# Attention of a two-layer transformer block: probabilities transposed by DMA as two 16-bit planes, and 16-bit values

## What is computed

```python
q = rope(rms_norm(x @ wq)); k = rope(rms_norm(x @ wk)); v = x @ wv          # 16 query heads, 4 key heads, 128 wide
k_full = concat(rms_norm(ctx @ wk_ctx), k); v_full = concat(ctx @ wv_ctx, v) # 512 keys, the last 256 causal
probs = softmax(q @ k_full.T / sqrt(128) + causal)
x = x + (probs @ v_full) @ wo
x = x + ffn0(layernorm(x)); x = x + topk_attention(...); x = x + gated_ffn(...)
```

## Time and profile before

| | |
|---|---|
| median of 3 runs | 1545.7 us (1543.1 to 1548.31) |
| profiled execution | 1547.26 us, span 1546.0 us |
| granted TensorE clock | 0.993 of full speed |
| PE busy | 1488.8 us, 96% |
| DVE busy | 1137.2 us, 74% |
| ACT busy | 959.3 us, 62% |
| POOL busy | 692.1 us, 45% |
| first attention | from the start to about 877 us |

### The profile page before, as it was taken

The page is one execution under the profiler, slowest core; times in us unless marked ns, Lnnn a source line. Parts: engine busy times, 40 slices in busy tenths (PEclk is TensorE's granted clock), DMA queues, the critical chain, the costliest instruction groups (busy, mean ns, idle before and its releaser), DMA issues. The chain is left out here.

```text
span 1546.0 us, 26210 instructions
## 1 busy us (share of the span) xinstructions
PE 1488.8 (96%) x8644; PEld 1165.6 (75%) x8644; DVE 1137.2 (74%) x2966; ACT 959.3 (62%) x2470; POOL 692.1 (45%) x832
## 2 busy tenths in 40 slices
PE   7899999999999999999999999999998899999988
PEld 6778888888888888888888666666666566666653
DVE  6787677777776877777788765555566898888774
ACT  5666666666666656666667765555546577666655
POOL 4564555464645555555567300000015455555544
PEclk9999999999999999999999999999999999999999
DMA  7011111111111111111144789778866301111000
GB/s 281 28 42 55 42 69 42 42 69 42 56 56 42 69 42 42 69 42 56 57 190 177 263 288 292 260 248 261 260 210 203 99 9 54 56 49 42 28 14 28
DMA packets 84327, 165.09 MB, mean 107 GB/s; under 512 B 39392, under 2 KB 39520, under 8 KB 82784
## 3 DMA queue, kind: packets, MB, share of 16 engines
q1 hardware_dynamic: 84192, 163.41, 30.8%
HBM read 113.05 MB, written 41.94 MB: 100 GB/s over the span
## 5 line engine op out<-in xcount | busy, mean ns | idle before, releaser
L617 ACT ACTIVATE Pt<-Pt,small 128x384 f32<-128x384 f32 (+1 forms) x256 | 172.7, 682 | 106.1 <-DVE small L877 106.0
L368 PE MATMUL bank<-wq,xT 128*128 128x512 f32 x768 | 206.7, 404 | 1.0 <-DVE wq L772 1.0
L421 PE MATMUL bank<-PT,vv 128*128 128x512 f32 x672 | 199.6, 405 | 4.7 <-DVE PT L862 3.8
L1135 POOL TENSOR_SCALAR Pt<-Pt,small 128x384 f32<-128x384 f32 (+1 forms) x256 | 164.0, 653 | 79.0 <-DVE small L885 78.9
L877 DVE CUSTOM_DVE_ANT_0 Pt<-quad,mask,small 128x384 f32<-128x384 f32 (+1 forms) x256 | 171.6, 679 | 30.7 <-PE quad L398 29.4
L1356 PE MATMUL bank<-wq,ot 128*128 128x512 f32 x768 | 182.1, 395 | 1.5 <-DMA ot<-ot_scratch 1.5
L862 DVE TENSOR_TENSOR PT<-quad,PT 128x512 fp32r<-128x512 f32 x224 | 153.6, 686 | 37.9 <-ACT PT L609 37.5
L1356 PEld LDWEIGHTS bank<-wq,ot 128*128 128x128 f32 x768 | 143.9, 188 | 33.7 <-DMA ot<-ot_scratch 2.2
L368 PEld LDWEIGHTS bank<-wq,xT 128*128 128x128 f32 x768 | 136.8, 189 | 26.4 <-DVE wq L772 2.3
L1123 POOL TENSOR_TENSOR t<-t 128x512 f32<-128x512 f32 x64 | 83.6, 1306 | 144.1 <-DVE t L843 144.1
L421 PEld LDWEIGHTS bank<-PT,vv 128*128 128x128 f32 x672 | 116.4, 189 | 28.9 <-DVE PT L862 10.2
(11 more groups left out here) (286 smaller groups left out, 3502.6 us busy)
## 6 DMA issues: line engine op xcount, KB each, us to landing
ot_scratch<-OT SPq DMA_DIRECT2D x64, 512.0 KB, 2.9
ot<-ot_scratch SPq DMA_DIRECT2D x64, 512.0 KB, 5.7
wkv_f<-in_w SPq DMA_DIRECT2D x12, 512.0 KB, 6.5
wkc_f<-in_w SPq DMA_DIRECT2D x12, 512.0 KB, 6.9
wkv_f<-in_wg SPq DMA_DIRECT2D x11, 512.0 KB, 6.9
wkv_f<-in_wd SPq DMA_DIRECT2D x11, 512.0 KB, 6.6
wkv_f<-in_wu SPq DMA_DIRECT2D x10, 512.0 KB, 7.1
stg<-in_ctxT SPq DMA_DIRECT2D x16, 256.0 KB, 4.1
```

The costliest lines, as they stand in the source:

```text
L368: ins = pe.matmul(bQ[:], xT[p][:, k, qt * 128:qt * 128 + 128], wq[j][:, g, k, :], start=(part == 0 and k == 0), stop=(part == 2 and k == 3))
L421: ins = pe.matmul(bO[:], vv[x][:, bg % 2, kt, :], PT[y][:, k % 2, :], start=(kt == 0 and n == 0), stop=(kt == tiles_in(i) - 1 and n == 2))
L617: act.activation(p, p, ACT.Exp, bias=nm[:, i % 2, h:h + 1], scale=-1.0, accum_out=sm[:, i % 2, h:h + 1]).then_inc(f["s_exp"], 1)
L1135: pool.tensor_scalar(p, p, ri[:, i % 2, h:h + 1], 1.0, ALU.mult, ALU.mult).then_inc(f["p_n"], 1)
```

## The change

The normalised probabilities are no longer transposed by TensorE. pool_norm now multiplies E (one buffer, where Pt had two) by 2^15 over the row sum and writes a float16 plane; dve_p_lo writes the remainder E times the same factor minus that plane as a second float16 plane, per head, both inputs in SBUF. For each block, SP issues one DMA transpose per plane for all heads (sp_p_turn: 12 or 16 tiles of 128 by 128) into PT. The two planes are one buffer each (planes), so pool_norm of a block's head 0 waits for t_hi, the landing of the block before's high transpose, and dve_p_lo of head 0 for t_lo, that of the low one. pe_pv then runs over the whole block in three parts, high plane first, low plane last. The values vv are float16 planes too, scaled per group by a factor sig that is worked out from the sums of squares of weights and of x's context (act_square, pe_scale, dve_scale, pool_scale, dve_unscale) at steps 0, 2, 4 and once per batch; act_o and dve_o_lo undo the scale. Scores rotate over three PSUM banks, bS, where there were two; the fourth bank of quad goes to even units of keys and values. Further: dve_k_n moves to ACT (act_k_n), dve_ln_b to POOL (pool_ln), dve_ri gets a second small instruction and a wait between the two, even and odd steps get one common order, dve_k_lo and dve_q stand at the end of dve_step behind the four dve_p_lo, and the product with the last attention blocks (pe_y) is placed anew around steps 62 and 63.

```diff
-    bS = [quad[:, 0, :], quad[:, 1, :]]
-    bP = [quad[:, 2, :], quad[:, 3, :]]
+    bS = [quad[:, j, :] for j in range(3)]
...
-    vv = [sb(st, f"vv{j}", [128, 2, 4, 128], F32R) for j in range(2)]
+    vv = sb(st, "vv", [128, 2, 2, 4, 128], F16)
...
-    Pt = [sb(st, "Pt0", [128, 4, 384], F32), sb(st, "Pt1", [128, 4, 512], F32)]
+    E = sb(st, "E", [128, 4, 512], F32)
+    PT = [sb(st, "PT0", [128, 24, 128], F16)]
...
+    def scales(i):
+        if i in (0, 2, 4):
+            return i // 2, 0, (0, 1, 2)[i // 2] + (i > 0), 2 if i == 0 else 1
+        return 2 + (i + 2) // 8, (i + 2) // 8, 0, 4
+    def scaled(i):
+        return i in (0, 2, 4) or i % 8 == 6 and i + 2 < NBLK
...
+    def sp_p_turn(i, x):
+        n = tiles_in(i)
+        if x == 0:
+            after(sp, f["pv_mm"], i - 1)
+        sp.wait_ge(f[("p_n", "p_lo")[x]], 4 * i + 4)
+        sp.dma_start_transpose(PT[i % 2][:, 4 * n * x:4 * n * x + 4 * n, :],
+                               planes[:, x, 0:4 * width(i)]).then_inc((t_hi, t_lo)[x], 16)
...
-        for i in range(1, NBLK + 1):
+        for i in range(NBLK + 2):
             b, r = divmod(i, 8)
-            p = i - 1
+            if i >= 2:
+                p = i - 2
+                sp.wait_ge(f["o_lo"], p + 1)
+                sp.dma_start(ot_dram[2 * (p // 8) + p % 2, p // 2 % 4], OT[:].bitcast(F32)).then_inc(f["ot0"], 16)
+            if i == 62:
+                sp.wait_ge(f["xt_mm"], NT)
+                sp.wait_ge(f["q_rope"], NBLK)
+                sp.wait_ge(f["k_rope"], NU // 2)
+                sp.wait_ge(f["q_mm"], NBLK)
+                sp.wait_ge(f["kv_mm"], NU)
+                sp.wait_ge(f["ot0"], 16 * 56)
+                for c in range(2):
+                    ffn["sp_ot"](c)
+            if i < NBLK:
+                for x in range(2):
+                    sp_p_turn(i, x)
...
+        if h == 1 and i and scaled(i - 1):
+            pe.wait_ge(f["v_scale"], 3 * scales(i - 1)[0] + 2)
+        after(pe, f["s_ev"], 4 * i + h - 2)
...
+    def pe_scale(i):
+        k, b, lo, n = scales(i)
+        bank = bank_s(i, 2)
+        pe.wait_ge(f["v_sq"], squares(k))
+        pe.wait_ge(f["s_ev"], 4 * i + 3)
+        after(pe, f["v_scale"], 3 * k)
+        for j in range(2):
+            pe.matmul(bank[:, 384:384 + n], ones[:], w_sq[:, j, lo:lo + n], start=(j == 0), stop=(j == 1))
+        for j in range(2):
+            ins = pe.matmul(bank[:, 388:389], ones[:], c_sq[:, j:j + 1], start=(j == 0), stop=(j == 1))
+        ins.then_inc(f["v_scale"], 1)
+    def pe_pv(i, part):
+        if i < 0:
+            return
+        n = tiles_in(i)
+        x, y = ((0, 0), (1, 0), (0, 1))[part]
+        if part == 0:
+            pe.wait_ge(f["v_lo"], max(2 * (i // 2) + 2, 3))
             after(pe, f["o_lo"], i)
-        for n, (x, y) in enumerate(PRODUCTS):
-            ins = pe.matmul(bO[:], vv[x][:, bg % 2, kt, :], PT[y][:, k % 2, :],
-                            start=(kt == 0 and n == 0), stop=(kt == tiles_in(i) - 1 and n == 2))
-        ins.then_inc(f["pv_mm"], 1)
+            pe.wait_ge(t_hi, 16 * (i + 1))
+        if part == 2:
+            pe.wait_ge(t_lo, T_LO + 16 * (i + 1))
+        heads = PT[i % 2][:].rearrange("p (x h k) q -> p x h k q", x=2, h=4)
+        for kt in range(n):
+            ins = pe.matmul(bO[:].rearrange("p (h q) -> p h q", h=4), vv[:, x, i // 2 % 2, kt, :], heads[:, y, :, kt, :],
+                            start=(part == 0 and kt == 0), stop=(part == 2 and kt == n - 1))
+        if part == 2:
+            ins.then_inc(f["pv_mm"], 1)
...
+    def pe_step(i):
+        turn = i % 8 == 6 and i + 2 < NBLK
         pe_s(i, 0)
         pe_s(i, 1)
+        if i == 0:
+            pe_q(1, 2)
+        if turn:
+            pe_x_turn(2 * (i // 8) + 2)
         pe_kv(i + 2)
...
+        if turn:
             pe_x_turn(2 * (i // 8) + 3)
         pe_s(i, 2)
         pe_s(i, 3)
-        pe_p_turn(i - 1, 2)
-        pe_pv(i - 1, 1)
-        pe_p_turn(i - 1, 3)
+        if turn:
+            pe_pv(i - 1, 0)
+            pe_pv(i - 1, 1)
         pe_q_turn(i + 1)
+        if scaled(i):
+            pe_scale(i)
         if i == 60:
             pe_w1_sum()
...
+        for part in range(3):
+            pe_q(i + 2, part)
         if i == 63:
             ffn["pe_y"](0, 1)
+        if not turn:
+            pe_pv(i - 1, 0)
+            pe_pv(i - 1, 1)
+        pe_k_turn(i + 2)
         pe_pv(i - 1, 2)
...
+        if i == 62:
+            pe.wait_ge(f["q_sq"], NBLK)
+            ffn["pe_y"](0, 0)
...
+    def act_k_n(u):
+        if u >= NU:
+            return
+        act.wait_ge(f["k_rs"], u + 1)
+        after(act, f["kt_mm"], u)
+        for t in range(2):
+            ins = act.activation(kn[:, t], kv4(u)[:, 0, t], ACT.Copy, scale=krs[:, t:t + 1])
+        ins.then_inc(f["k_n"], 1)
...
+    def act_c_square(c):
+        b, t = divmod(c, 2)
+        act.wait_ge(f["c_hi"], c + 1)
+        if c in (2, 3):
+            act.wait_ge(f["v_scale"], 7)
+        act_square(c if b == 0 else 8 + c, cT[0][:, :, t * 128:t * 128 + 128], c_sq[:, t:t + 1])
...
+    def act_step(i):
         turn = i % 8 == 6 and i + 2 < NBLK
-        act_p_hi(i - 1, 1)
-        act_q_sq(i + 1)
-        if i in (2, 4):
+        if i == 0:
+            act_w_hi(6)
+        act_o(i - 2)
+        if i:
+            act_v_hi(i + 1)
+            act_q_sq(i + 1)
+        if 1 <= i <= 4:
             act_w_hi(2 * i + 6)
-        if i < 61:
-            act_last(i, 0)
         act_exp(i, 0)
         act_exp(i, 1)
+        if i == 0:
+            act_q_sq(1)
         act_k_sq(i + 2)
         if turn:
             act_x_hi(2 * (i // 8) + 2)
             act_x_hi(2 * (i // 8) + 3)
...
         act_last(i, 0)
         act_exp(i, 2)
-        if i > 1:
-            act_p_hi(i - 1, 2)
+        act_k_n(i + 2)
         act_exp(i, 3)
+        if i == 0:
+            act_w_hi(7)
+        elif i <= 4:
+            act_w_hi(2 * i + 7)
         act_q_hi(i + 1)
-        if i == 61:
-            act_last(i, 1)
-        act_o(i - 1)
+        if i == 0:
+            act_v_hi(0)
+            act_v_hi(1)
+        act_k_hi(i + 2)
         if i in (1, 3):
...
+            act_w_square(2 + i // 2)
+        if i % 8 == 4 and i + 4 < NBLK:
+            for m in (2 * (i // 8) + 2, 2 * (i // 8) + 3):
+                act_c_hi(m)
+                act_c_square(m)
+        act_last(i, 1)
+        act_last(i, 2)
...
+    def dve_scale(i):
+        k, b, lo, n = scales(i)
+        bank = bank_s(i, 2)
+        dve.wait_ge(f["v_scale"], 3 * k + 1)
+        dve.tensor_scalar(f_v, bank[:, 388:389], 512.0, BOUND, ALU.add, ALU.mult)
+        dve.tensor_scalar(w_v[:, 0:n], bank[:, 384:384 + n], 1e-30, None, ALU.max).then_inc(f["v_scale"], 1)
+    def dve_unscale(i):
+        k, b, lo, n = scales(i)
+        dve.wait_ge(f["v_scale"], 3 * k + 3)
+        dve.reciprocal(unsig[:, b % 2, lo:lo + n], unsig[:, b % 2, lo:lo + n])
...
+    def dve_p_lo(i, h):
+        dve.wait_ge(f["p_n"], 4 * i + h + 1)
+        if h == 0:
+            after(dve, t_lo, T_LO + 16 * i if i else 0)
+        dve.scalar_tensor_tensor(plane(i, 1, h), E[:, h, 0:width(i)], ri[:, i % 2, h:h + 1], plane(i, 0, h),
+                                 ALU.mult, ALU.subtract).then_inc(f["p_lo"], 1)
...
+        r = ri[:, i % 2, 2 * p:2 * p + 2]
+        v.did(dve.reciprocal(r, sm[:, i % 2, 2 * p:2 * p + 2]))
+        v.settle()
+        dve.tensor_scalar(r, r, FULL, None, ALU.mult).then_inc(f["s_ri"], 1)
...
+    def dve_step(i):
         turn = i % 8 == 6 and i + 2 < NBLK
-        if not turn and i != 62:
+        dve_ev(i, 0)
+        dve_ev(i, 1)
+        if i == 0:
+            dve_w(5)
+            dve_q(1)
+        dve_o_lo(i - 2)
+        if i:
             dve_v_lo(i + 1)
...
         dve_q_ve(i + 1)
-        dve_p_lo(i - 1, 1)
-        if i == NBLK:
-            mem["dve_ternary"](0, 2)
         dve_ri(i, 0)
-        dve_k_ss(i + 2)
-        dve_last(i, 0)
-        if i == 16:
-            dve_co()
         if turn:
             dve_x_lo(2 * (i // 8) + 2)
+        if i == 0:
+            dve_w(6)
+        dve_last(i, 0)
         dve_ev(i, 2)
         if turn:
             dve_x_lo(2 * (i // 8) + 3)
-        if i == 62:
-            dve_p_lo(i - 1, 2)
+        dve_k_ss(i + 2)
+        dve_p_lo(i, 0)
         dve_ev(i, 3)
-        if i in (2, 4):
+        if scaled(i):
+            dve_scale(i)
+        dve_p_lo(i, 1)
+        if 1 <= i <= 4:
             dve_w(2 * i + 6)
...
         dve_ri(i, 1)
         dve_q_lo(i + 1)
+        if i == 0:
+            dve_w(7)
+        dve_p_lo(i, 2)
+        dve_p_lo(i, 3)
+        if i % 8 == 5 and i + 3 < NBLK:
+            dve_ln_a(2 * (i // 8) + 2)
+            dve_ln_a(2 * (i // 8) + 3)
+        if scaled(i):
+            dve_unscale(i)
+        if i == 0:
+            dve_v_lo(0)
+            dve_v_lo(1)
+        if 1 <= i <= 4:
+            dve_w(2 * i + 7)
+        if i == 16:
+            dve_co()
         dve_last(i, 1)
...
         dve_k_lo(i + 2)
```

(38 more changed lines are left out.)

434 lines of the change are left out of this document (84 added, 350 removed).

## The result

The changed kernel takes 1653.2 us (median of 4), the kernel before 1546.1 in the same job: 1.0708 times, 95% interval 1.0655 to 1.076. So it is 107 us slower. The forecast was 30 us slower, and the time lies outside the range of 1512 to 1640. The profiled execution has a span of 1649.4 us.

The account below looks back on a forecast made before the run. TensorE bounds the kernel before; after the change, chains of waits between VectorE and GpSimd set odd steps. Pairs -14, batches +25, start +9, last steps +17 and tail -5 give +32: forecast 1576 us, range 1512 to 1640.

Parts of the forecast that it names:

- the walk through the odd step: Ordinary odd step: chain of VectorE and GpSimd instructions added up from the first score matmul, ending with low keys at 13.6 us.
- The even step: Ordinary even step: TensorE's own 11.2 us plus 0.3 from waiting for the low plane's transpose, 11.5 us.
- The pair: Ordinary odd and even step together: 25.1 us against 25.53 before, -14 us over 32 pairs.
- The value matmul's 0.22 us: Value matmuls in 16 bit follow each other by 0.22 us instead of 0.233, some 0.16 to 0.2 per step.
- the waits of both engines for each other: VectorE instructions with two SBUF inputs and GpSimd's run one after the other; without these waits the odd step takes 12.35 us.
- the landings cover themselves: DMA transposes land before TensorE wants them; only the even step's first low plane waits, about 0.3 us reaching the step's end.
- The rival that gave 1645: Slow landings of 16-tile transposes hold the next block's dve_p_lo: at 7.6 us, 2.1 more a pair, +67 us; chance 0.17.
- the batch, +3.55 taken: Steps preparing a batch: layer norm, casts, turns of x and scaling cost 5.55 against 2.0 before, +25 us over seven.
- the last steps, +15.5 taken: Steps 56 to 62: w1 sums some 6.6 and pool_wo 10.4, together +17, less 1.5 from the shorter pairs.
- the start, +10.8 taken: Steps 0 to 7: weight splits and early scalings +9, a batch +3.5, pairs -1.7; nothing ahead of step 0.
- The tail, -5 taken: From step 63: seven groups of transposes and filler go, but the last transposes have little cover; -5, between -10 and +5.
- my rivals: Overlap without port waits 1536 (0.20), TensorE full 1425 (0.08), slow landings 1645 (0.17), in between 1550 (0.13).

Follow-up runs that it names:

- e3: Changed kernel with dve_p_lo writing E times the factor without subtracting the high plane, so one SBUF input instead of two: 1603.3 us.
- e18: e16 with all four high planes formed on GpSimd again: 1569.9 us.
- e2: Changed kernel with 14 and 11 extra 16-bit matmuls without a reader filling TensorE's idle at the end of a batch's steps 5 and 7: 1633.3 us.
- e1: Changed kernel with the loads of w1 and wo in blocks 56, 58 and 60 issued ahead of the DMA transposes: 1640.0 us.
- e16: Kernel with several edits combined (1549.1 us); in steps 0 to 4 query-weight casts and the first queries' sum moved earlier: 1533.5 us.
- e6: Changed kernel with the layer norm's subtract and multiply moved back from GpSimd to VectorE, behind dve_q of step 5: 1649.5 us.
- e5: Changed kernel with the high planes of heads 2 and 3 formed by ScalarE instead of GpSimd: 1591.6 us.
- e7: Changed kernel with, in steps 1 to 4, ScalarE's even weight cast behind two exponentials and VectorE's odd remainder ahead of the last two low planes: 1645.5 us.

## Why the prediction was wrong

**Right: the walk through the odd step.** From the first score matmul at 511.42, mine against the trace: rotation left over 1.4 / 1.8; roots of the queries 4.9 / 5.35; planes 0 and 1 6.3 / 6.7; root of the keys 7.4 / 7.8; norm 7.95 / 8.5; rotation 10.6 / 10.9; planes 2 and 3 12.0 / 12.3; low planes 13.2 / 13.5; low keys 13.6 / 13.8. The even step is TensorE's, 10.92 (mine 11.2 + 0.3). The pair is 24.8 (25.1) where the clock is full, and from 200 to 711 us TensorE is busy for 449.8 us, 88% as forecast. The value matmul's 0.22 us and the waits of both engines for each other (e3) held too.

**Right: the landings cover themselves.** The rival that gave 1645, the number nearest to the time, rested on slow landings; VectorE and GpSimd wait 4.9 us for them. Its nearness is chance. In e18, where the rest is faster, low planes wait 18.6 us for transposes.

**Wrong: the batch, +3.55 taken, +9.15 measured.** (Steps 8 to 55: +36.4 and 24 pairs at -0.77 make 54.9 for six.) Steps 5 and 7 were right: 16.75 and 15.2 against 16.9 and 15.1. The step of the prediction that failed is the price of the steps behind them, which I took as TensorE's own 11.2, plus 0.8 for the turns of x in one of them. In that sum every TensorE instruction had its duration at full clock, while the same text made 5.8 and 4.3 us of idle ahead of it (16.75 and 15.2 less 10.9; measured 5.3 and 3.5). The kernel before has no such idle and a clock of 1.00 in all of the earlier trace rows. Over the six batches the forecast is 33.6 us short. The lower clock is 24 of these in the steps that e2 restores and 3.0 in steps 36 and 52, and pe_scale, which I priced on GpSimd but not on TensorE, is 0.81 in each, 4.9 in all. e2 as a whole returns 20 us, since in it other steps lose their clock.

**Wrong: the last steps, +15.5 taken, +33.6 measured.** The second step that failed: I priced the w1 sums as instructions and did not follow sp_last past the transposes on SyncE's queue, which puts its loads one step later. e1 returns 13 of the missing 18; the other 5 were not taken apart.

**Wrong: the start, +10.8 taken, +30.2 measured** (with what lies ahead of step 0). The third: I counted VectorE's two instructions per step and not ScalarE's casts, whose late place holds TensorE's queries, nor the lower clock in these steps (a mean of 0.85 from step 0 to 7). The casts are not all of it: in these steps of the changed kernel TensorE waits 6.1 us for them, 6.2 for the rotated keys, 4.5 for the low keys and 3.6 for the queries' sum. e16, which moves the casts and that sum, returns 14 us in steps 0 to 7, from another base. 2.4 of the 5.2 us ahead of step 0 are the layer norm's multiply, 2.08 us on GpSimd, which I had not priced at the start (e6).

**The tail, -5 taken, +3.2 measured**, within the bounds of -10 and +5; not tested. This is one trace against one: from step 63 on those of the experiments take 695.7 to 702.3 us, and e3's 690.9, against 697.6 for the changed kernel.

Together the misses are 19.4 + 25.4 + 18.1 + 8.2 = 71 us, and with the +32 of the forecast this is the 103. None of my rivals had the clock, the late loads or the casts. Each of these three misses alone is larger than the 13 us by which the time passes the end of the range.

Not settled: why the clock fell behind some ordinary odd steps and not behind others with the same idle, and how the 62 us of e5 split between the port and the queue.

## What to carry over

A change that frees the bounding engine gives it idle time, and the matmuls behind that idle can be slower than every row of the old trace: price the steps behind a gap at the lower clock too. Filling one gap can show the lower clock elsewhere, so count all steps and not the mended ones. When an operation is put on a queue, walk every entry behind it, loads for later stages included. Gains of single edits on one chain don't add up: 125 us of single gains were 81 together.

## What the hardware showed

- VectorE's TENSOR_SCALAR on 128 x 2 numbers (L879, 75 times from 200 to 711 us) takes 0.17 us with no GpSimd instruction beside it, 0.73 beside GpSimd's product of 128 x 256, whose end it shares, and 1.2 beside its sum of 128 x 512. I had followed only instructions with two SBUF inputs. The same section of the Trainium skill's page "SBUF — State Buffer" counts a TENSOR_SCALAR without accumulator among those that can take the shared port; these rows and e3's, where the form with an accumulator kept to 743 ns, agree. Beside GpSimd's root on 128 x 4 it stayed at 0.17 to 0.20 in 28 cases.
- GpSimd's TENSOR_SCALAR on 128 x 512 takes 0.70 us with one factor per row and a constant, 2.08 us with two numbers per row; VectorE does the second in 0.53 (fastest, before; the median is 0.97).
- Of two transposes issued one behind the other, the first lands 3.8 us after its issue with 12 tiles and 4.4 with 16, the second 4.1 and 4.9 (medians of 32 each); an issue holds SyncE for 1.8 us (median; 1.3 to 6.7).
- The two steps of a batch that have 5.3 and 3.5 us of TensorE idle were followed by stretches of 1.2 GHz (mean clock 0.77 to 0.87 in all fourteen steps behind them in the changed kernel). Behind ordinary odd steps with 2.24 us of idle the clock held in ten of twelve cases and fell to a mean of 0.86 in two, in e2 in seven of twelve. In e7 it held behind 3.5 us too, in steps 8 and 24. So about the same idle was followed by either, and a step behind a gap has two prices.
